# Layer 0's router in another order: one-hots with experts innermost, values by 16-bit masks, reciprocal straight from PSUM

## The reference, cut to what matters

```
tf    = sigmoid(sum(time_emb))                 # one number per batch
decay = exp(-exp(w)) * (0.5 + 0.5 * tf)
ek    = exp(min(k, 30));  ekv = ek * v         # v is k
forward and backward scans of ekv and ek over the 256 tokens: a = a * decay + src
euk   = exp(min(u + k, 30))
num   = nf + nb - ekv + euk * v;  den = df + db - ek + euk
cond  = sigmoid(x) * (num / max(den, 1e-8)) * (0.8 + 0.2 * tf)
```

## Time and profile before

| | |
|---|---|
| median of 3 runs | 620.84 us (620.84 to 621.14) |
| the profiled execution | 620.28 us, its span 618.5 us |
| busy: PE, DVE, ACT, POOL | 490.7, 415.4, 213.9, 302.3 us |
| TensorE's granted clock, mean | 0.873 of full speed |
| chain that ended last | PE 56%, DVE 14%, POOL 10%, issue 8%, DMA 8% |

### The profile page before, as it was taken

The page is one execution under the profiler, slowest core; times in us unless marked ns, Lnnn a source line. Parts: engine busy times, 40 slices in busy tenths (PEclk is TensorE's granted clock), DMA queues, the critical chain, the costliest instruction groups (busy, mean ns, idle before and its releaser), DMA issues.

```text
span 618.5 us, 8996 instructions
## 1 busy us (share of the span) xinstructions
PE 490.7 (79%) x2758; PEld 332.5 (54%) x2758; DVE 415.4 (67%) x803; ACT 213.9 (35%) x543; POOL 302.3 (49%) x262
## 2 busy tenths in 40 slices
PE   1867622889999999889999997899999992378863
PEld 1554421667878786645665474356676471234423
DVE  6998996599999999638786477478751568211003
ACT  2310040323222223315656243155554241145442
POOL 4106922779999941044774200347676100457750
PEclk9968755799999999699999985999999975588886
DMA  8400010599955510364676559447333401689935
GB/s 229 94 4 32 0 35 18 147 252 244 256 168 146 162 36 1 119 161 137 215 227 212 181 171 320 112 119 226 123 98 94 162 2 68 202 275 324 305 121 203
DMA packets 84927, 92.78 MB, mean 150 GB/s; under 512 B 8370, under 2 KB 64274, under 8 KB 84882
## 3 DMA queue, kind: packets, MB, share of 16 engines
q1 hardware_dynamic: 75858, 67.56, 36.7%
q0 software_dynamic: 9024, 24.65, 13.5%
HBM read 72.79 MB, written 19.40 MB: 149 GB/s over the span
## 4 chain that ended last, share of the span: by engine, by line
PE 56%; DVE 14%; POOL 10%; issue 8%; DMA 8%; ACT 2%; SPq 1%; DVEq 0%; POOLq 0%; ACTq 0%
PE y_ps L630 10%; PE g_ps L760 7%; PE u_ps L603 5%; PE u_ps L724 5%; PE g_ps L724 4%; POOL R L1643 4%; DMA xs<-ctab,idx_g 4%; PE y_ps L694 3%; PE g_ps L685 3%; PE y_ps L521 3%; PE r_ps L707 3%; POOL ybuf L1689 3%; PE g_ps L618 3%; PE u_ps L676 2%; PE r_ps L745 2%
## 5 line engine op out<-in xcount | busy, mean ns | idle before, releaser
L1682 POOL DMA_INDIRECT xs<-ctab,idx_g x76 | 75.9, 999 | 145.2 <-DVE idx_g L1322 114.8
L1689 POOL DMA_INDIRECT ybuf<-o_s,idx_s x76 | 77.4, 1019 | 66.2 <-ACT o_s L946 56.9
L1650 POOL DMA_INDIRECT xg<-ctab,idx x36 | 54.2, 1504 | 30.0 <-DVE idx L1463 22.5
L630 PE MATMUL y_ps<-P,o_hi 128*128 128x512 f32 x144 | 59.9, 416 | 0.2 <-DVE o_lo L1484 0.2
L630 PE MATMUL y_ps<-P,o_lo 128*128 128x512 f32 x144 | 56.6, 393 | 0.0
L707 PE MATMUL r_ps<-ident_s,xs 128*128 128x128 f32 x152 | 33.6, 305 | 19.5 <-DMA xs<-ctab,idx_g 13.7
L1346 DVE TENSOR_TENSOR h_s<-a_s 128x128 f32<-128x128 f32 x24 | 7.0, 292 | 59.7 <-ACT a_s L932 44.5
L946 ACT ACTIVATE o_s<-g_ps 128x256 f32<-128x256 f32 x76 | 29.1, 383 | 42.9 <-PE g_ps L760 30.2
L924 ACT ACTIVATE xT_s<-r_ps 128x256 f32<-128x256 f32 x76 | 28.9, 380 | 42.4 <-PE r_ps L707 41.5
L707 PEld LDWEIGHTS r_ps<-ident_s,xs 128*128 128x128 f32 x152 | 18.6, 149 | 42.4 <-DMA xs<-ctab,idx_g 21.4
L603 PE MATMUL u_ps<-xT_g,wup 128*96 128x96 f32 x384 | 37.8, 253 | 0.5 <-DVE hT L1478 0.5
(11 more groups left out here) (255 smaller groups left out, 1103.2 us busy)
## 6 DMA issues: line engine op xcount, KB each, us to landing
wR<-w SPq DMA_DIRECT2D x48, 256.0 KB, 4.0
wup<-in_wglu SPq DMA_DIRECT2D x36, 256.0 KB, 3.9
ysb<-ybuf SPq DMA_DIRECT2D x6, 1024.0 KB, 6.8
wR<-in_wglu SPq DMA_DIRECT2D x4, 1216.0 KB, 10.3
wdn<-in_wglu SPq DMA_DIRECT2D x12, 384.0 KB, 4.9
raw_q<-in_wq SPq DMA_DIRECT2D x16, 256.0 KB
w<-w3o SPq DMA_DIRECT2D x16, 256.0 KB, 2.4
ctab<-ysb SPq DMA_DIRECT2D x6, 512.0 KB, 3.1
```

The lines of the kernel that those rows point to most:

```text
L630: mm = pe.matmul(y_ps[:, m, hf, :], o[:, b, m * P:(m + 1) * P], P1[:, b, hf * HALF:(hf + 1) * HALF], start=first and n == 0, stop=last and ...
L1650: pool.indirect_dma_start(out=xg[:, j % XG, :], out_offset=None, in_=ctab, in_offset=bass.IndirectOffsetOnAxis(ap=idx[:, j:j + 1], axis=0) ...
L1682: pool.indirect_dma_start(out=xs[:, n % XB, :], out_offset=None, in_=ctab, in_offset=bass.IndirectOffsetOnAxis(ap=idx_g[:, b:b + 1], axis= ...
L1689: pool.indirect_dma_start(out=ybuf, out_offset=bass.IndirectOffsetOnAxis(ap=idx_s[:, b:b + 1], axis=0), in_=o_s[:, n % OB, :], in_offset=N ...
```

## The change

Four parts.

- `finish0`: the reciprocal reads den from PSUM itself, and the product takes min(1/den, 1e8) in place of max(den, 1e-8) before. The scale by `oscale` is a ScalarE copy in place (`scale0`), and `cond(0, hf)` waits for four more of them.
- The one-hot `A` is laid out per group of 4 experts as (offset, expert), experts innermost, and compared with a table `iota_a` of the same layout. The rows of the lists then come in the order (offset, expert). `idx` stays in it; `move_x` puts the columns back to (expert, offset) as it reads PSUM; `gate0` and `tokf` are put back by one matmul with a permutation `swap` that ScalarE makes early.
- `route_values`: for each block a 16-bit mask (one compare of 192 elements), then a product of mask and values, in place of the combined compare and product.
- GpSimd makes three of the six sums u + k, with their bound at 30. ScalarE makes the other exponentials from `fs` with u as bias, and the bound, now exp(30), joins the subtraction in `wkv_part`.

```diff
             def finish0(o):
-                sums = y_ps[:, o % 2, 1, :]
-                invert(o, o % 2, sums)
-                ratio(o, UNIT0[o], o % 2, sums)
+                sums, inv = y_ps[:, o % 2, 1, :], fwd[:, o % 2, 1, :]
+                dve.wait_ge(num_ready, o + 1)
+                dve.reciprocal(inv, sums[:, NT:2 * NT]).then_inc(inv_ready, 1)
+                dve.wait_ge(inv_ready, o + 1)
+                dve.scalar_tensor_tensor(out=unit(R, UNIT0[o]), in0=inv, scalar=1e8, in1=sums[:, 0:NT],
+                                         op0=ALU.min, op1=ALU.mult).then_inc(ratio_ready, 1)
...
+            def scale0(o):
+                act.wait_ge(ratio_ready, o + 1)
+                q = UNIT0[o]
+                act.activation(unit(R, q), unit(R, q), ACT.Copy, scale=oscale[:, q:q + 1]).then_inc(R0_ready, 1)
...
             def cond(layer, hf):
+                if layer == 0:
+                    dve.wait_ge(R0_ready, UNITS // 2 * (hf + 1))
...
-                dve.tensor_reduce(mask4[:, :], ident_s[:, :].rearrange("p (e a) -> p e a", e=EG), AX, ALU.add)
+                dve.tensor_reduce(mask4[:, :], ident_s[:, :].rearrange("p (a e) -> p e a", e=EG), AX, ALU.add)
+                dve.tensor_copy(iota_a[:, :, :], iota_s[:, 0:AG].unsqueeze(2).to_broadcast([P, AG, EG]))
...
-                    dve.tensor_tensor(A[:, i % TH, :, :], iota16[:, 0:AG].unsqueeze(1).to_broadcast([P, KEPT, AG]),
-                                      off16[:, i, :].unsqueeze(2).to_broadcast([P, KEPT, AG]), ALU.is_equal
-                                      ).then_inc(A_ready, 1)
+                    dve.tensor_tensor(A[:, i % TH, :, :, :], iota_a[:, :, :].unsqueeze(1).to_broadcast([P, NGR, AG, EG]),
+                                      off16[:, i, :].rearrange("p (g e) -> p g e", e=EG).unsqueeze(2)
+                                      .to_broadcast([P, NGR, AG, EG]), ALU.is_equal).then_inc(A_ready, 1)
...
                 for k in range(BG):
-                    ins = dve.scalar_tensor_tensor(
-                        out=B[:, hf, k, :, :, :].rearrange("p v i e -> p v (i e)"),
-                        in0=blk16[:, half, :].rearrange("p i e -> p (i e)").unsqueeze(1)
-                        .to_broadcast([P, NV, TH * KEPT]),
-                        scalar=float(k), in1=values, op0=ALU.is_equal, op1=ALU.mult)
+                    ins = dve.tensor_scalar(own[:, k, :], blk16[:, half, :].rearrange("p i e -> p (i e)"), float(k), None,
+                                            ALU.is_equal)
+                ins.then_inc(own_ready, 1)
+                dve.wait_ge(own_ready, hf + 1)
+                for k in range(BG):
+                    ins = dve.tensor_tensor(B[:, hf, k, :, :, :].rearrange("p v i e -> p v (i e)"), values,
+                                            own[:, k:k + 1, :].to_broadcast([P, NV, TH * KEPT]), ALU.mult)
...
+            def swap_rows():
+
+                pe.wait_ge(seen_ready, 1)
+                pe.wait_ge(swap_ready, 1)
+                pe.matmul(u_ps[:, 0:2 * NCH], swap[:, :], seen2[:, :, :].rearrange("p v j -> p (v j)"), start=True, stop=True,
+                          skip_group_check=True).then_inc(swapped, 1)
...
+                pe.wait_ge(gate0_ready, 1)
                 wait(pe, hT_ready, 2 * g + pair)
...
                 act.activation(xT_g[:, g % 2, :, :, b * AG:(b + 1) * AG],
-                               r_ps[:, 0:KT * P].rearrange("p (k e a) -> p k e a", k=KT, e=EG), ACT.Copy
+                               r_ps[:, 0:KT * P].rearrange("p (k a e) -> p k e a", k=KT, e=EG), ACT.Copy
                                ).then_inc(xT_ready, 1)
...
-                dve.tensor_scalar(tokf[:, :], seen[:, :], -1.0, None, ALU.add)
                 dve.tensor_scalar(idx[:, :], seen[:, :], -1.0, 0.0, ALU.add, ALU.max).then_inc(idx_ready, 1)
-                link(dve.tensor_tensor(gate0[:, :], L[:, :, 3], L[:, :, 4], ALU.add))
-                dve.tensor_tensor(gate0[:, :], gate0[:, :], L[:, :, 2], ALU.add).then_inc(gate0_ready, 1)
+                link(dve.tensor_tensor(seen2[:, 0, :], L[:, :, 3], L[:, :, 4], ALU.add))
+                dve.tensor_scalar(seen2[:, 1, :], seen[:, :], -1.0, None, ALU.add)
+                dve.tensor_tensor(seen2[:, 0, :], seen2[:, 0, :], L[:, :, 2], ALU.add).then_inc(seen_ready, 1)
+                dve.wait_ge(swapped, 1)
+                dve.tensor_copy(tokf[:, :], u_ps[:, NCH:2 * NCH])
+                dve.tensor_copy(gate0[:, :], u_ps[:, 0:NCH]).then_inc(gate0_ready, 1)
...
-            for layer in range(1, NL):
-                add_u(layer)
+            for layer, kt in ((1, 0), (1, 1), (2, 0)):
+                add_u(layer, kt)
```

More of the change, by code:

```diff
@@ L189, in build @@
                 B = sbr("B", [P, 2, BG, NV, TH, KEPT], BF16)
-                A = sbr("A", [P, TH, KEPT, AG], BF16)
+                A = sbr("A", [P, TH, NGR, AG, EG], BF16)
+                own = sbr("own", [P, BG, TH * KEPT], BF16)
                 M = sbr("M", [P, NCH * NV, EG])
@@ L521, in add @@
                     return pe.matmul(dst, diagonal[:, :], src, start=start, stop=stop, skip_group_check=True)
-                wait(pe, R_ready, 3 * (o - 1))
+                wait(pe, ratio_ready, o - 1)
                 pe.wait_ge(eukv_ready, o + 1)
@@ L966, in exp_uk @@
             def exp_uk(layer):
-                act.wait_ge(uk_more, layer)
-                e = R[:, RL[layer]:RL[layer] + UNITS, :]
-                act.activation(e, e, ACT.Exp).then_inc(euk_ready, 1)
+                for kt in range(KT):
+                    q = RL[layer] + kt * NB
+                    e = R[:, q:q + NB, :]
+                    if 2 * layer + kt < 5:
+                        act.wait_ge(uk_more, 2 * layer + kt - 1)
+                        ins = act.activation(e, e, ACT.Exp)
+                    else:
+                        ins = act.activation(e, fs[:, kt * NB:(kt + 1) * NB, :], ACT.Exp, bias=wus[:, layer, 1, kt:kt + 1])
+                ins.then_inc(euk_ready, 1)
+            def scale0(o):
+                act.wait_ge(ratio_ready, o + 1)
+                q = UNIT0[o]
+                act.activation(unit(R, q), unit(R, q), ACT.Copy, scale=oscale[:, q:q + 1]).then_inc(R0_ready, 1)
             def move_x(g, b):
@@ L1012, in _ @@
                            ).then_inc(gwp_ready, 1)
+            for o in range(1, UNITS // 2):
+                scale0(o)
             for hf in range(2):
@@ L1016, in _ @@
                 route_rows(hf)
+                if hf == 0:
+                    for o in range(UNITS // 2, UNITS):
+                        scale0(o)
             for layer in range(1, NL):
@@ L1087, in scans, with invert, ratio @@
                 last.then_inc(scan_ready, 1)
[L1089 to L1094, removed]
+            def invert(q, buf):
+                dve.wait_ge(num_ready, q + 1)
+                den, o = fwd[:, buf, 1, :], q - UNITS
+                dve.tensor_scalar(den, den, 1e-8, None, ALU.max).then_inc(R_ready, 1)
                 dve.wait_ge(R_ready, o * 3 + 1)
                 dve.reciprocal(den, den).then_inc(R_ready, 1)
-            def ratio(o, q, buf, sums=None):
+            def ratio(q, buf):
+                o = q - UNITS
                 dve.wait_ge(R_ready, o * 3 + 2)
-                dve.scalar_tensor_tensor(out=unit(R, at_R(q)), in0=fwd[:, buf, 0, :] if sums is None else sums[:, 0:NT],
+                dve.scalar_tensor_tensor(out=unit(R, at_R(q)), in0=fwd[:, buf, 0, :],
                                          scalar=oscale[:, bass.ds(q, 1)], in1=fwd[:, buf, 1, :],
@@ L1367, in wkv_part @@
                     if ph == 0:
-                        link(dve.tensor_tensor(d, unit(R, at_R(q)), unit(ek, q % UNITS), ALU.subtract))
+                        link(dve.scalar_tensor_tensor(out=d, in0=unit(R, at_R(q)), scalar=E30,
+                                                      in1=unit(ek, q % UNITS), op0=ALU.min, op1=ALU.subtract))
                     else:
@@ L1637, in tables, with add_u @@
                 ins.then_inc(iota_ready, 1)
-            def add_u(layer):
-                for kt in range(KT):
-                    q = RL[layer] + kt * NB
-                    ins = pool.tensor_scalar(R[:, q:q + NB, :], fs[:, kt * NB:(kt + 1) * NB, :],
-                                             wus[:, layer, 1, kt:kt + 1], 30.0, ALU.add, ALU.min)
-                ins.then_inc(uk_more, 1)
+            def add_u(layer, kt):
+                q = RL[layer] + kt * NB
+                pool.tensor_scalar(R[:, q:q + NB, :], fs[:, kt * NB:(kt + 1) * NB, :],
+                                   wus[:, layer, 1, kt:kt + 1], 30.0, ALU.add, ALU.min).then_inc(uk_more, 1)
             def gather(g, b):
```

19 lines of the change are left out of this document (16 added, 3 removed).

## The result

| | before | after |
|---|---|---|
| median | 620.84 us | 611.02 us (609.19, 610.53, 611.52, 616.51) |
| profiled execution, its span | 620.28, 618.5 us | 610.53, 608.7 us |
| busy: PE, DVE, ACT, POOL | 490.7, 415.4, 213.9, 302.3 us | 494.8, 401.4, 219.3, 288.1 us |

The account below looks back on a forecast made before the run. Layer 0's router was taken as bound by VectorE, the expert loop by TensorE. Savings of 1.75 + 7.37 + 1.78 + 0.09 = 10.99 us took 620.28 to 609.3, plus 0.56 for the median: 609.9 us (80% range 607.3 to 614.5).

Parts of the forecast that it names:

- Part 1: Layer 0's router: reciprocal straight from PSUM, scale moved to ScalarE; claimed to save 2.30 - 0.55 = 1.75 us.
- 1.38 at 36.72: Layer 0's router: saving claimed by unit 3's finish, 0.92 us from an earlier start plus its own 0.46.
- the upper end of 1.0 us: Unit finishes: a reciprocal reading PSUM might cost 0.12 us more each, 8 x 0.12 = 1.0 us; not taken.
- unit 2's saving would only lengthen unit 3's wait: Layer 0's router: unit 3 waits for TensorE, so the third 0.46 us saving only makes that wait longer.
- Part 2: Router's eight slot one-hots: two elements per cycle saves 6.53 us, less GpSimd interference 0.84 us, together 7.37 us.
- (a): Rival on one-hots: four-element rows don't pair, rows of 192 do; gain 4.46 us, 616.4 us, chance 0.09.
- (b): Rival on one-hots and values: neither gets the fast form; gain 1.40 us, 619.4 us, chance 0.04.
- Part 3: Router's values: masks and fast products in place of combined operations, 0.89 us per half, 1.78 us for both.
- Part 4: The rest: indices issued 0.09 us earlier; permuted gates and token numbers covered, strided PSUM reads taken as costing 0.
- (c): Rival in the expert loop: VectorE becomes its bound, 12 groups each 1.04 us longer; 621.4 us, chance 0.04.
- (d): Rival: layout works, but ScalarE wait, PSUM reads and first block cost 1.0 + 0.4 + 0.5 us; 611.8 us, chance 0.13.
- its mirror: Rival in the router: a stall of TensorE shrinks with the shift, 1.5 us better; 608.4 us, chance 0.08.

Follow-up runs that it names:

- gate copies first: The changed kernel with ScalarE's permutation and first scale moved behind the two gate copies: 611.85 us, in a later run 609.08 us.
- the last runs: The changed kernel and three variants reordering ScalarE's and VectorE's work, six runs each on one chip: medians 611.01, 609.08, 605.97 and 604.10 us.
- the best version here: The kernel with slots early, plus the first half's gates moved ahead of unit 4's finish: 608.52 us, in a later run 604.10 us.
- slots early: The kernel with gate copies first, plus the first half's slot positions moved ahead of unit 7's finish: 607.65 us, in a later run 605.97 us.

## Why the prediction was right

The forecast of 609.9 us (607.3 to 614.5) stands 1.1 us from the measured 611.02, and by its sum it was right in three parts and wrong in the first.

- **Part 1, the step that failed**: "TensorE's sums for unit 2 start 0.7 us later and end near 29.2 us, before VectorE asks at 30.0". They start 0.78 us later, as worked out, but the term took the durations of before, at the upper clock level, without asking whether that level would hold behind a longer idle time. At the lower one they end near 31.0 us. VectorE also asked at 29.49 and not at 30.0. What the prediction called 1.38 at 36.72 was 0.06, and part 1 gave 0.25 us for 1.75. Over five traces of this code `cond(0, 1)` starts at 68.31 to 71.85, against 69.83 in the one trace of before: a gain of 1.5 us at best, where the level held, and a loss of 2.0 at worst. Why the level fell in four of the five stays open. With the gate copies first, 2.3 us are there at `weigh(1)`, more than the 1.38.
- The sizes within part 1 were right: the reciprocal from PSUM 1.75 us like that from SBUF, so the upper end of 1.0 us falls; the product 0.42 us instead of 0.48; the wait for ScalarE's last scale 0.57 us (0.55), in every trace of the new finish. The claim that unit 2's saving would only lengthen unit 3's wait shows with the gate copies first: 0.83 to 0.95 us there in four traces, before 0.39.
- **Part 2**: 7.23 us for 7.37. The doubt about four-element rows, in (a) and (b), is settled by the 952 ns of one. This is what the Trainium skill ("VectorE: DVE Perf Modes", Mode 2×_1P) states, and both sides of it show here: 952 ns with 16 bits everywhere, 6.76 us for four with one f32 input.
- **Part 3**: 2.0 us for 1.78; removing it cost 2.04.
- **Part 4**: the gates and token numbers by the permutation are hidden, and the strided reads of PSUM take 382 ns against 381. The Trainium skill's warning on cachelines ("SBUF — State Buffer") is said of matmuls; for ScalarE's reads by a step of 16 bytes this trace shows no cost.
- **(c)**, VectorE as the bound of the loop, falls: from the first gather to the first sums into x it is 138.70 us before, 138.51 after, and 138.18 to 138.53 in all four of the last runs. Its 621.4 us is also added up wrongly: 609.9 and 12.5 are 622.4.
- **(d)** lies near the result by its number, 611.8, and not by its mechanism: the wait for ScalarE, the reads of PSUM and the strided moves stayed at the values taken. Nor did its mirror come: the stall at unit 4 is 2.36 us in both traces.

So the total came out near because the two large terms were right, 9.2 us of the 11.0. That it came within 1.1 us has luck in it: part 1 is worth anything from 1.5 to -2.0 us by the trace that one takes. The miss of 1.4 us at the indices has a cause that the prediction had named elsewhere (TensorE at half its clock) but not at the place where the change lengthened its idle time. Its 1.2 us for what a measurement can tell from none is too small as well: the interval of the result is 2.4 us to either side.

## What to carry to other kernels

Lay out a 16-bit two-input VectorE operation so that every operand has step 1 innermost, even if the rows have only four elements; a broadcast may stand one dimension out, and a combined compare-and-multiply is worth splitting. A small instruction put ahead of one that TensorE waits for can cost more than its length: 0.5 to 0.7 us here for 0.7 us of work, and in four traces of five TensorE's next matmuls also ran at half the clock, 1.7 us and more on top. Put it behind. Where an engine waits for another in a fixed place, move work from the path behind it into the wait; by the medians this gave 5.0 of the 6.9 us by which the best version here beats the changed kernel.

## What the hardware showed that was not expected

Whether TensorE's clock falls behind an idle stretch isn't told by the stretch alone: 1.82 us were followed by the lower level after and by the upper one with the slots early, 2.41 and 2.11 us by the upper one, and the same code took both ways in different executions.

A product of GpSimd can hold up a scan of VectorE that starts beside it. GpSimd and VectorE before, and with the gate copies first (its second trace):

```profile
28.75 1.05 POOL L1629 TENSOR_TENSOR dif<-R,fs 128x256 f32<-128x256 f32 x1 [4.53 <-PE y_ps L521]
```

```profile
29.21 1.15 DVE L1084 TENSOR_TENSOR_SCAN fwd<-decay,ek 128x256 f32<-128x256 f32 x1
```

```profile
28.86 0.78 POOL L1679 TENSOR_TENSOR dif<-R,fs 128x256 f32<-128x256 f32 x1 [5.45 <-PE y_ps L529]
```

```profile
27.87 0.66 DVE L1121 TENSOR_TENSOR_SCAN fwd<-decay,ek 128x256 f32<-128x256 f32 x1
...
29.03 1.73 DVE L1189 RECIPROCAL fwd<-y_ps 128x256 f32<-128x256 f32 x1
```

Before, scan and product overlap and take 1.15 and 1.05 us; once the finish is shorter, the product meets mostly the reciprocal and takes 0.78, the scan 0.66. So the four scans of unit 3 take 2.35 us (26.68 to 29.03) and not 2.84 (28.02 to 30.86): 0.5 of the 0.9 us by which `weigh(1)` gained more than the 1.38.

The reciprocal is not held up, and not because it reads PSUM: the one from SBUF wasn't either. Before, with GpSimd's six sums around it:

```profile
58.43 1.75 DVE L1096 RECIPROCAL fwd<-fwd 128x256 f32<-128x256 f32 x1
```

The one at 20.13 began beside a product of GpSimd and the one at 25.71 beside an idle GpSimd; both took 1.75 us as well.
